# Another order for four merged streams in a language-model tower with a selective scan and a mixture of experts

## The reference

```
h = emb[x] + pos                       # token gather
x1, x2 = h, 0                          # two reversible layers
for l in range(2):
    y1 = x1 + lsh_attention(layer_norm(x2), Wqk[l], Wv[l], Wo[l])
    y2 = x2 + gelu(layer_norm(y1) @ W1[l] + b1) @ W2[l] + b2
    x1, x2 = y1, y2
h = h_in + tower(...)                  # (x1 + x2) / 2
# selective scan in both directions, 256 inner channels, 16 states
def step(h, (u_t, dt_t, B_t, C_t)):
    dA = exp(dt_t[..., None] * A)
    h = dA * h + (dt_t * u_t)[..., None] * B_t
    return h, einsum('bds,bs->bd', h, C_t)
x = ln(x + mamba_fwd(x) + flip(mamba_bwd(flip(x))));  x = ln(x + ffn(x))
# mixture: top 2 of 8 experts, all computed and weighted with comb (0 where not chosen)
for e in range(8):
    out = out + comb[:, e:e+1] * (gelu(x @ w1[e] + b1[e]) @ w2[e] + b2[e])
# then a layer of attention with 8 heads, and a layer of three small MLPs (and, or, xor) on nibbles
```

## Time and profile before

| | |
|---|---|
| time, median of 3 runs | 3891.53 us (3889.09 to 3901.82) |
| profiled execution: time | 3896.18 us |
| its span, first to last instruction | 3893.9 us |
| instructions | 31221 |
| mean granted TensorE clock | 0.887 |
| HBM traffic | 103 GB/s over the span |
| ACT_TABLE_LOAD at L705 and L701 | x516 and x232 |

### The profile page before, as it was taken

The page is one execution under the profiler, slowest core; times in us unless marked ns, Lnnn a source line. Parts: engine busy times, 40 slices in busy tenths (PEclk is TensorE's granted clock), DMA queues, the critical chain, the costliest instruction groups (busy, mean ns, idle before and its releaser), DMA issues.

```text
span 3893.9 us, 31221 instructions
## 1 busy us (share of the span) xinstructions
PE 3127.3 (80%) x8728; PEld 1368.3 (35%) x8728; DVE 3420.1 (88%) x4654; ACT 2925.3 (75%) x3806; POOL 1337.2 (34%) x644
## 2 busy tenths in 40 slices
PE   5655878889787788979888888979788887877797
PEld 3231423334343333424343333424343333432232
DVE  1499979999898999999999999999999998999822
ACT  2546887987868888787888878787888879686442
POOL 0254333333323334343433443343433433333200
PEclk8757788989888899989999999989989999888797
DMA  1233333424324243333434342343424333333310
GB/s 63 77 108 96 113 109 92 128 80 135 99 94 118 93 131 95 119 118 109 125 98 123 107 131 94 121 117 109 124 95 126 104 116 104 104 119 104 100 49 11
DMA packets 209022, 404.60 MB, mean 104 GB/s; under 512 B 25936, under 2 KB 34256, under 8 KB 208592
## 3 DMA queue, kind: packets, MB, share of 16 engines
q1 hardware_dynamic: 206800, 398.41, 32.8%
q0 software_dynamic: 2048, 4.20, 1.0%
HBM read 387.57 MB, written 14.94 MB: 103 GB/s over the span
## 4 chain that ended last, share of the span: by engine, by line
PE 37%; DVE 26%; ACT 25%; issue 12%; POOL 0%; DMA 0%; DVEq 0%; ACTq 0%; POOLq 0%
PE bank_a L569 8%; DVE states L921 7%; PE bank_b L580 7%; ACT L705 6%; DVE states L927 6%; ACT decay L705 6%; DVE y_sum L932 3%; ACT L701 3%; ACT tok L705 3%; ACT last L705 3%; ACT middle L705 3%; PE bank_p L478 1%; PE bank_c L397 1%; PE bank_p L421 1%; PE bank_c L640 1%
## 5 line engine op out<-in xcount | busy, mean ns | idle before, releaser
L1199 POOL TENSOR_TENSOR dbu<-dtu,b_rows 128x1024 f32<-128x1024 f32 x512 | 1243.4, 2431 | 2104.1 <-DVE states L921 1823.6
L921 DVE TENSOR_TENSOR_SCAN states<-decay,dbu 128x512 f32<-128x512 f32 x1024 | 1298.7, 1311 | 38.1 <-ACT decay L705 30.5
L705 ACT ACTIVATE decay<-dt,neg_a 128x508 f32<-128x508 f32 x1024 | 659.4, 707 | 64.6 <-DVE states L921 59.0
L705 ACT ACT_TABLE_LOAD x516 | 662.0, 1283 | 47.5 <-PEq L344 16.6
L569 PE MATMUL bank_a<-middle,experts 128*128 128x512 f32 x1024 | 616.2, 687 | 97.1 <-ACT middle L705 88.9
L705 ACT ACTIVATE middle<-bank_a,columns 128x512 f32<-128x512 f32 x608 | 417.8, 687 | 329.6 <-PE bank_a L569 305.4
L927 DVE TENSOR_TENSOR states<-states,c_rows 128x512 f32<-128x512 f32 x960 | 610.8, 679 | 0.3
L932 DVE TENSOR_TENSOR y_sum<-y_sum,states 128x512 f32<-128x512 f32 x960 | 609.9, 674 | 0.2
L580 PE MATMUL bank_b<-middle,experts 128*128 128x512 f32 x1024 | 572.7, 643 | 21.4 <-ACT middle L705 11.8
L705 ACT ACTIVATE last<-bank_c 128x512 f32<-128x512 f32 (+2 forms) x320 | 201.0, 634 | 198.0 <-PE bank_c L617 52.4
L701 ACT ACT_TABLE_LOAD x232 | 297.7, 1283 | 46.0 <-PE bank_p L469 17.0
(11 more groups left out here) (206 smaller groups left out, 3944.7 us busy)
## 6 DMA issues: line engine op xcount, KB each, us to landing
b_rows<-bc_scratch SPq DMA_DIRECT2D x512, 256.0 KB, 3.4
c_rows<-bc_scratch SPq DMA_DIRECT2D x512, 256.0 KB, 3.3
experts<-ew SPq DMA_DIRECT2D x128, 512.0 KB, 3.5
comb_rows<-comb_scratch SPq DMA_DIRECT2D x128, 256.0 KB, 3.8
h_scratch<-tok SPq DMA_DIRECT2D x16, 256.0 KB, 3.3
x_scratch<-xin SPq DMA_DIRECT2D x16, 256.0 KB, 3.8
xr<-x_scratch SPq DMA_DIRECT2D x16, 256.0 KB, 4.9
h<-h_scratch SPq DMA_DIRECT2D x16, 256.0 KB, 5.3
```

What stands on the lines that cost most here:

```text
L705: return nc.scalar.activation(out, in_, func, **more)
L921: tick(nc.vector.tensor_tensor_scan(hs[:, h, ::step], da[:, n % DECAYS, h, ::step], dbu[:, n % AHEAD, h, ::step], 0.0, ALU.mult, ALU.add), ...
L1199: tick(nc.gpsimd.tensor_tensor(dbu[:, n % AHEAD], dtu[:, k % 2], row, ALU.mult), "a_dbu")
```

## The change

Only the strings in `ORDER` differ, for all five engines. Every letter occurs as often as before, so all instructions of the program stay except table loads, which follow from ScalarE's order. The new strings came from exchanging neighbouring letters, starting at the present ones. Letters that differ: TensorE 754 of 2836, ScalarE 523 of 2261, VectorE 606 of 2823, GpSimd 46 of 546, SP 427 of 1317. ACT_TABLE_LOADs in the program: 748 before, 737 in the change. Of the diff one line of TensorE's string is shown, which has no more to tell than the others:

```diff
 ORDER = {
     "passes": 0,
     "PE": (
-        "PDCPPPPPPPPPPPPCPPPPPPPPPPPPPPPPPPPPPPPPPPPPPPPPPPPDDDPDCPDPDPPDDPDDPPDPPDPPPPPPPPPPPPPPPPPPPPPPPPPP"
+        "PPPPPPPPDPCPPPPPPPPPCPPPPPPPPPPPPPPPPPPPPPPPPPPPPPPDDDPDPDPCDPPDDPPPDDDDPPPPPPPPPPPPPPPPPPPPPPPPPPPP"
...
```

More of the change, by code:

```diff
@@ L50 @@
[L50 to L54, removed]
@@ new lines @@
+        "PCPCCCPCCPPCCPPCPPCCPCCCPPDCDCDCDCPCCDPCCDCCPPCDCCDCPCPPDPCCCPPCPDPCCCCPCCCDPDCPPPDDCCCDCCCDDDCCDDDP"
+        "DCDPCPDPDDCPDCPDPDDCDPCCCCCDCCCDCCDCCCPDCDCCDCDPCCPCCDPPCDCCPPDCCPDCCCDDCCCDCCPCCPDDPPCDCDPCPCDCPPCC"
+        "CPPPCCPCCPPDCCDCDDCPCCDCDCPCPCCCDDPCPCCPCDCDCPPDPDPCPCCDDCCDCCPPDDDDPDCDDPPCDPDCDDDCDDCDDPPPCDDDCCCP"
+        "DCCDCCPCDPCPDPCCPCCDPPDCCPPCCPCCDCCCPCCCDPCDCCCDPDCDPDCPCPCDCCDDCCPCPCPCCPPCCPCCPPPCCPDCCDCDCCPDPCDC"
+        "DCCCPPCCDCDDPCDPCPPCCPPCCCDPDPCPDCDCCCCDCPCPDDCDPPDCDDDCDDCDDCDDDDDCCCPCCPPDCCDPDPCDCPPDCCDPDCCCPCCD"
@@ new lines @@
+        "CPPDPPPCCCDPCCCCCDPDDPCCCCPCDCCPCDDPPCDCCCCCPDCCPDPCPPPCCPPCCPCDCDCDCPCDCPCDCCDCPCPCCDCCDPPCDCDPPCPC"
+        "CPCDPDPCPCCCDDCCCCDPPDCPPDDDDCDDCDDCDDDCDCCCDCPDCDPPCCPDCDCCPCCCDPPDCCPDPCCDCCDCCCPCDPPDPCCPPDCCPDCC"
+        "DCCDCCDCPDCPCDPCCPCCCDDDPCCPPCCPPCPCPPCCCCPPDCCDDCDPCCCDCCDCPPCCCDDPDDPCPPCCCPPPCDPCCDPCPCDDPCCDCPPP"
+        "CDDDDCDDCDDCDCDDPDCCCDPCDDCCCPDPPPPCCDCDCCPCCCDCCDCPCDCCDPPDCCPPDCCPPDCCPDPCCCPCCCDPCDCCCDDPDDPCCPPC"
+        "CDPPCCDCPDPCPCCPCCPCCDCCDCDCDPCCDCCDCPPCCDDCPDDPPCPCPCCPCPDPCCCDPPCDDPCCDCPPPDCDDDCDDDCDCDCDDPDCPCCD"
@@ new lines @@
+        "CCDDCPCPDPPPCCDCDCCCPDCCCCDCCCPCDDPPDCCPPDCCPPDCCPDPCCPCDCCCPCDDCCDCPDDPCCPPCCDPCDCPCDCPPPCCCPCPCCDC"
+        "CDDCCDPCCDCCDCCPPDDCPCDDPCPPCCPCPPCDPCDCCCPPDDPCCDPPCPDCDDDCDDDCDCDCDDPDCCCPDCCDPCCDDPPPPCCDCCDCCPDC"
+        "CCCDCCCCPDDPPDCCPPDCCPPDCCPDPCPCCDCCCPCDCPDDCCDPDCCPPCCDPPCCDPCPDCPCCCPCPCCDCDDCCDPCCCDCCDCPCPCDDCPD"
+        "DPCPPPCCCPCPPDCDCPCPCDDPCDPCCPCDDPDDCDDCDDCDCDDPDCCPDCCCDCCPDDPPPPCCDCCCDCPCDCCCDCPCCCDDPPDCPPCDCCPD"
+        "PCCPDPCPCCDCCCPCDCCDCDPDDPCPPCCCDPPCCCDPDCPPCCPCCPCCDCCCDCDDCCDPCCDCCPPCCDPDDDPPCCPCCPPPCDPCCDPCCPDD"
@@ new lines @@
+        "PCCDPCPPDCDDDCDDDCDCDCDPDDCCPDCCCDCPDDPPPPCCCDCCDCCPDCCDCCCPCCDDPPCDCCPPDCCPPDCCPDPCCPCDCCPCCDCCCDDP"
+        "DDPCCPPCCDPCCDCCPDPPPCCPCCPCCDCCDCDCDPCCDCDCCPCPPCDDDCPDCPCPCPPPCCDPCCCDCPPDDPDCPPCCPDCDDDCDDDCDCDCD"
+        "PDDCCPDCCCDCPCPDPDPPCCDCDCPCCCDCCCCPDCCCDPPDDCPCPDCCPPDCCPDPDCPCCPCCCCDCDPDCCDDPCCPPCCDPPCCCDDPPCPCP"
+        "CCCPCDCCCDDCCDPCCDCDCPCPCCDDPDDCPCPPPCCPCPCDPCCDCCPPDDPCDCPCPPDCDDDCDDDCDCDCDPDDCCPCDCDCCCPDPDPPPCCD"
+        "CCDCCPCDCCCDCPCCDCDPPDCCPPDCCPPDCCPDPCCPCCDCCPCDDCDCCPDDPCCPCDCPPCCDCDPCPPPCCPCCCCPDCCDDCDCPCCDCCDCC"
@@ L167 @@
+        "AAAACCDAAAAAAACAAAAACPAACDCAPAAAACAAAAAAAAAAAAAAAAAADAAACAAAACAACAAACAAAACAAACAAAAAACAAACAAAAACCAACA"
+        "AACAAADCCCCCDCCCD",
         "",
```

167 lines of the change are left out of this document (75 added, 92 removed).

## The result

The change is slower: a median of 3957.89 us (3951.35 to 3958.64, 4 runs) against 3890.31 us of before, a ratio of 1.0162, interval 1.0142 to 1.0182, so 55 to 71 us and 63 at the middle. The forecast was 3878.7, and even the rival that ended on the slow side stopped at 3915.

What follows compares the result with a forecast made beforehand. The prediction took VectorE's own work to set the time wherever the other engines feed it. Its five terms summed to -12.8 us, from the 3891.53 us median to 3878.7, with a range of 3852 to 3903.

Steps and rivals of the forecast that it cites:

- Term 1: Start of direction 4: fewer ScalarE table loads ahead of the first decays bring the scans earlier, -5.6 us.
- Term 2: Start of direction 8: two u become neighbours and share a table load on ScalarE, -0.7 us.
- Term 3: Prologue: L516, 0.86 us on the chain, goes behind L379, -0.9 us.
- Term 4: VectorE beside GpSimd: L1113, L1079 and L1155 moved away from dbu run shorter, -8.6 us.
- Term 5: SP's row transfers and GpSimd's token gather come later in their lists, a loss of +3 us.
- rival (b): Slower: on SP's in-order list, waiting transfers hold back c_rows and the scans; 3895 to 3915 us, chance 0.17.
- rival (a): No measurable change: dbu savings fall on neighbours, direction 4's stall is passed on; 3887 to 3892 us, chance 0.30.
- rival (c): Larger gain: a sixth off VectorE's L580 and decay waits and off scan slowdown beside GpSimd; 3851 us, chance 0.08.

Runs made afterwards that it cites:

- e6: Only GpSimd's string changed against the kernel before: median 3894.71 us, ratio 1.0010 (0.9990 to 1.0030).
- e11: Only VectorE's L1113 at its new places, against the kernel before: median 3897.82 us, ratio 1.0003 (0.9988 to 1.0018).
- e4: Only GpSimd's and SP's strings changed against the kernel before: median 3920.53 us, ratio 1.0078 (1.0047 to 1.0109).
- e1: All strings but SP's changed against the kernel before: median 3962.34 us, ratio 1.0175 (1.0152 to 1.0198).
- e7: Only VectorE's token and beside stream steps at their new places, against the kernel before: median 3916.58 us, ratio 1.0051.
- e10: Only those VectorE steps that come earlier among the scans moved, against the kernel before: median 3915.31 us, ratio 1.0060.
- e5: Only VectorE's string changed against the kernel before: median 3946.81 us, ratio 1.0129 (1.0094 to 1.0164).
- e2: TensorE's, ScalarE's and VectorE's strings changed against the kernel before: median 3966.28 us, ratio 1.0169 (1.0131 to 1.0203 not used; difference +66 us).

## Why the prediction was wrong, point by point

**The step that failed** is the sentence "Sum: -5.6 - 0.7 - 0.9 - 8.6 + 3 = -12.8": it has no term for the 361 VectorE instructions that changed their place among the scans, most by one, and that hardly any of the five terms counted. The prediction called ScalarE's loads slack "where scans follow each other without a wait", said of the steady stretch that it has "3% idle, which an order can touch little", and asked of each move only whether it removed a wait that was there. It did not ask how much spare time each trip through TensorE or ScalarE had. In the trace of before the trip that ends at L992 in direction 7 had 0.3 us to spare, and the move took 3.6 of it (1.28 and 2.34). That term, by VectorE's string alone, is +50 us (37 to 64), some 30 of it at a like clock by the estimate behind e6. The trace of before could have priced it: a scan pair of 2.4 us against the spare of a trip.

**Term 1, direction 4** was forecast as first scan 551.9, second 562.0, -5.6 net. In the changed kernel:

```profile
537.25 0.69 DVE L896 TENSOR_TENSOR tok<-bank_p,tok 128x512 f32<-128x512 f32 x1 [0.64 <-ACT tok L705]
...
557.64 0.75 DVE L1106 SCALAR_TENSOR_TENSOR middle<-bank_b,columns,comb_rows 128x512 f32<-128x512 f32 x1 [15.04 <-PE bank_b L580]
...
559.03 2.34 DVE L921 TENSOR_TENSOR_SCAN states<-decay,dbu 128x512 f32<-128x512 f32 x2
...
569.62 2.35 DVE L921 TENSOR_TENSOR_SCAN states<-decay,dbu 128x512 f32<-128x512 f32 x2 [7.07 <-ACT decay L705]
```

The shape was right: the first scan early (559.03 for 562.87), the second held by ScalarE's loads, 10.6 us later where 10.1 was forecast. The start was not: L896 came at 537.25, not 2.2 us before 535.02. ScalarE's tok before it ended only at 537.22, as ScalarE itself stood 1.20 us for L410, and its second u stood 2.92 us for L399. The second scan pair ended at 572.0, 2 us after that of before (569.9), but by the start of direction 5 the two kernels were level (679.0 and 678.9). So the term is about 0 over the direction, and the item count that I trusted took ScalarE's inputs as always there.

**Term 2, direction 8**: forecast -0.7; L1106 waited 16.50 where it had waited 15.21, and the decays behind it 2.40 where it was 1.39, so it was a loss of 2.3. **Term 3**: the first scan came at 162.3 for 162.9, -0.6 for a forecast of -0.9, which is right.

**Term 4** was the largest gain, -8.6. VectorE's busy time did fall by 11.2 us, L1113's mean from 762 to 737 (near 720 was forecast) and L1079's from 498 to 322. The two together are 5.6 us (25 x 112 and 176 x 16), and the rest may be the difference between traces that e6 shows. In e11, L1113's move by itself saved nothing of L1113 (775) and gained no time, which is the bound 0 of the term. By the Trainium skill, SBUF — State Buffer, section "Who interferes with whom", the engine that issues first gets the shared ports for the whole instruction and the other waits. What the trace shows agrees as far as it goes: dbu's mean went from 2431 to 2445 ns in both e11 and the change, 7 us over 512. Whether that is VectorE's surplus, passed on, was not shown.

**Term 5** was +3 for SP and the gather. The gather's part is nothing that can be told (e6). SP's part is larger by itself than my +3, up to 30 us (e4), with the mechanism of rival (b), seen at 961 us; in the whole change it adds nothing to VectorE's (e1). Rival (b) named the right sign and a real mechanism, and the wrong engine for this loss. Its own sum was wrong as well: 23.5 for the rows and the same for the gathers, less 16, is +31 or 3923, not +24 and 3915. In rival (a), -4.2 holds the +3 already, so "-4.2 + 3" counts it twice, and the lower end of the range, 3852, is rival (c)'s value and not half way to it. None of the three reaches the 3957.89. Of what would have shown the forecast wrong, a wait that names c_rows (4.1 us), "L1106's wait on L580 above 115.7" and "dbu's mean up while L1113's falls" came. The wait on L580 alone is a poor sign: it is 106.2 in e7 and 108.3 in e10, which are slower too. Rival (c) had its chance on the idea that an order can only pick up what is left; here it gave more away.

**What stays open**: TensorE's and ScalarE's own share. Their new strings run only with VectorE's new one. With it they bring 50 to 66 (e5 and e2), and the intervals overlap, so it is between nothing and some 35 us. Open too is how much of each loss is the lower clock, and what lowers it. Which producers the 63.5 us at unmoved instructions belong to was not settled either; one trip was followed.

## What to carry to other kernels

Where engines work fixed lists, a busy share of 88% on one engine does not mean that the others always have time to spare. Before moving a step past another in such a list, find the trip that ends at it and the one that starts from it, through the other engines, and compare the spare time in front and behind with the length of what it is moved past; here one scan pair (2.4 us) was more than the 0.3 us that was to spare. Price the many moves by one place, not only those at the long stalls, and count time saved on a busy engine only when the wait that follows it does not grow by as much. The spare time depends on TensorE's clock as well: the same trip took 15.7 us in one trace and 14.3 in another. If a list was found by a search, change it engine by engine on the chip: the loss of one engine can hide in that of another, so that taking one back may gain nothing.

## What the runs showed of the hardware that was not expected

GpSimd's dbu costs the scans in single hits. In the trace of before 67 of 1024 scans took over 1.4 us (the median is 1215 ns, the longest 4058), and each of the 67 overlaps a dbu; 113 other scans overlap one and stay below 1.4 us. In e11, where 53 adds of 0.68 us stand elsewhere and no scan moved, the scans' mean is 1299 ns for 1311. That is one trace of each, and with VectorE's list unchanged the mean was 1306 (e4) and 1307 (e6), so it is not shown that the moves did it.
